# Four graph layers on one core: the second layer's projections as products of rounded halves and rests

## What is computed

```
h = relu(layernorm(x)); x = x + attention(h, adj)            # first layer: q, k, v, softmax
h = relu(layernorm(x)); x = x + gated(h, adj)                # second layer, below
h = relu(layernorm(x)); x = x + (adj != 0) @ (h @ W + b) / deg
h = relu(layernorm(x)); x = x + masked_attention(h, adj)
```

```
hs = h @ W_sa;  s_left = hs @ a_sa[0,:256];  s_right = hs @ a_sa[0,256:]
e = where(adj != 0, exp(-leaky_relu(s_left[:,None] + s_right[None,:], 0.01)), 0)
x_a = (e / (sum(e, 1) + 1e-5)) @ hs
x_b = adj @ (h @ W_gcnb) + b_gcnb
out = sigmoid(alpha_a * x_a + alpha_b * x_b)     # alphas: sigmoids of adj @ h and h times a vector
```

## Time and profile before

| | |
|---|---|
| median of three runs | 398.59 us |
| the profiled execution's own time | 398.4 us |
| its span, first to last instruction | 396.6 us |
| TensorE matmul busy | 384.1 us (97%) |
| TensorE weight load busy | 353.3 us (89%) |
| VectorE busy | 336.8 us (85%) |
| ScalarE busy | 251.8 us (63%) |
| GpSimd busy | 121.8 us (31%) |
| mean granted TensorE clock | 0.998 of full speed |

### The profile page before, as it was taken

One profiled execution on the slowest core, in us unless ns is written; L12 is line 12 of the kernel. 1 busy time (PEld: TensorE's weight loads), 2 busy tenths in 40 slices (PEclk: granted clock), 3 DMA queues, 4 the chain that ended last, 5 costly groups with the idle time before them and its releaser, 6 DMA issues. The chain is left out here.

```text
span 396.6 us, 7768 instructions
## 1 busy us (share of the span) xinstructions
PE 384.1 (97%) x2651; PEld 353.3 (89%) x2651; DVE 336.8 (85%) x771; ACT 251.8 (63%) x531; POOL 121.8 (31%) x130
## 2 busy tenths in 40 slices
PE   7999999999999999999999999999999999999895
PEld 6888888999899899999999899998887898989874
DVE  6898899999984857999999989666888888799893
ACT  3553799888895657876787892255241566267772
POOL 1290000001010424322161011061010599379973
PEclk9999999999999999999999999999999999999999
DMA  8995000000000001000000000000000000010011
GB/s 238 380 382 173 0 0 2 2 0 2 0 2 0 2 1 55 2 2 0 3 2 0 3 0 2 2 1 2 0 2 0 0 2 2 0 55 1 2 54 37
DMA packets 10319, 13.99 MB, mean 35 GB/s; under 512 B 660, under 2 KB 7208, under 8 KB 10280
## 3 DMA queue, kind: packets, MB, share of 16 engines
q1 hardware_dynamic: 9736, 12.96, 9.6%
q10 hardware_dynamic: 544, 0.52, 0.4%
HBM read 12.10 MB, written 1.39 MB: 34 GB/s over the span
## 5 line engine op out<-in xcount | busy, mean ns | idle before, releaser
L1639 PE MATMUL ps<-v_hi,p_hi 128*128 128x258 f32 (+3 forms) x242 | 64.1, 295 | 0.3 <-DVE x_sb L1016 0.2
L402 POOL TENSOR_TENSOR mr_all<-mr_all,mhalf 128x4 f32<-128x4 f32 (+1 forms) x12 | 13.5, 1123 | 162.8 <-DVE mr_all L911 162.8
L1640 PE MATMUL ps<-v_lo,p_hi 128*128 128x258 f32 (+3 forms) x242 | 61.0, 281 | 0.0
L1639 PEld LDWEIGHTS ps<-v_hi,p_hi 128*128 128x128 f32 (+3 forms) x242 | 44.7, 185 | 2.1 <-issue 0.9
L1640 PEld LDWEIGHTS ps<-v_lo,p_hi 128*128 128x128 f32 (+3 forms) x242 | 44.7, 185 | 0.6
L1644 PE MATMUL ps<-v_hi,p_lo 128*128 128x258 f32 (+3 forms) x242 | 40.1, 283 | 1.1 <-DVE p_lo L1192 1.1
L998 DVE TENSOR_TENSOR s_sb<-s_sb,ps 128x512 f32<-128x512 f32 (+3 forms) x63 | 38.3, 610 | 1.3 <-PE ps L1626 1.3
L443 POOL TENSOR_TENSOR mid_lo<-adjT_sb,mid_hi 128x512 fp32r<-128x512 f32 (+2 forms) x16 | 22.6, 1412 | 48.3 <-ACT mid_hi L684 48.3
L1644 PEld LDWEIGHTS ps<-v_hi,p_lo 128*128 128x128 f32 (+3 forms) x242 | 32.5, 185 | 1.7 <-DVE p_lo L1192 1.6
L1931 PE MATMUL ps<-big_hi,p_lo 128*128 128x256 f32 (+3 forms) x121 | 31.8, 294 | 0.6 <-ACT p_lo L867 0.5
L1639 PE MATMUL ps<-big_hi,mid_hi 128*128 128x258 f32 (+3 forms) x121 | 31.8, 294 | 0.0
(11 more groups left out here) (252 smaller groups left out, 1218.1 us busy)
## 6 DMA issues: line engine op xcount, KB each, us to landing
adjT_sb<-in_adjT_dram SPq DMA_DIRECT2D x1, 2816.0 KB, 16.7
adjT_sb<-in_adjT_dram SPq DMA_DIRECT2D x3, 768.0 KB, 8.6
adjT_sb<-in_adjT_dram SPq DMA_DIRECT2D x1, 1815.0 KB, 21.3
out_dram<-x_sb SPq DMA_DIRECT2D x10, 128.0 KB
x_sb<-in_x_dram SPq DMA_DIRECT2D x2, 256.0 KB, 3.6
x_sb<-in_x_dram SPq DMA_DIRECT2D x1, 512.0 KB, 3.9
adjT_sb<-in_adjT_dram SPq DMA_DIRECT2D x1, 512.0 KB, 10.9
rows_sb<-in_rows_dram SPq DMA_DIRECT2D x1, 385.0 KB, 11.1
```

The lines of the kernel that those rows point to most:

```text
L1639: pe.matmul(out_ap, left_[0][0:k, n % RING, mine], right_[0][0:k, j, 0:cols_], start=(j == 0), stop=False)
L1640: pe.matmul(out_ap, left_[0][0:k, n % RING, mine], right_[1][0:k, j, 0:cols_], start=False, stop=False)
```

## The change

The split form replaces `project_full`. `h_hi` and `h_lo`, which the first and fourth layers use, now serve the second layer too: ScalarE writes the rounded half of each turned block into the place where `h_mid` was (`mid_lo`), and VectorE writes the rest into `mid_hi`, where T was. A turn and a projection now wait for the rest (`hlo`) in place of ScalarE's copy. On VectorE the eleven rests stand at step 36 (behind `add_out(1)`, `running` and `stats`), at 38 to 40, at 43 to 46, and in the written-out list. ScalarE splits both weight matrices at step 12, GpSimd writes their rests ahead of `norm(1, 0)`. The first three `adj_hi` wait for projections of h, since they overwrite blocks of rests.

```
--- before.py
+++ after.py
@@ -176,6 +176,7 @@
         rb = sb("rb", [P, NB])
 
         hT0 = [t[:, 0:C * N].rearrange("p (c n) -> p c n", c=C) for t in (big_hi, big_lo)]
+        h1 = [t[:, :].rearrange("p (b c n) -> p b c n", b=NB, c=C) for t in (mid_lo, mid_hi)]
         hT3 = [t[:, :, :].rearrange("p b w -> p (b w)")[:, 0:C * N].rearrange("p (c n) -> p c n", c=C) for t in (v_hi, v_lo)]
         g = [t[:, :].rearrange("p (b w) -> p b w", w=W) for t in (big_hi, big_lo)]
         tT = [t[:, 0:C * N].rearrange("p (c n) -> p c n", c=C) for t in (mid_hi, mid_lo)]
@@ -256,6 +257,8 @@
 
         def h_block(b, layer):
 
+            if layer == 1:
+                return [t[:, b, :, 0:rows(b)] for t in h1]
             return [t[:, :, b * P:b * P + rows(b)] for t in (hT3 if layer == 3 else hT0)]
 
         ps = ctx.enter_context(nc.psum_tensor("ps", [P, 8, BANK], F32))
@@ -285,7 +288,7 @@
             sem(n) for n in ("col_set", "uw_set", "gram_set", "wlr_set", "wext_set"))
         whi, wlo = sems("whi", 7), sems("wlo", 7)
         st, mv, veps, rstd, ln = (sem(n) for n in ("st", "mv", "veps", "rstd", "ln"))
-        zd, zt, hhi, hlo, h_set = (sem(n) for n in ("zd", "zt", "hhi", "hlo", "h_set"))
+        zd, zt, hhi, hlo = (sem(n) for n in ("zd", "zt", "hhi", "hlo"))
         x_add = sems("x_add", 4)
         t_mm, t_hi, t_lo = sems("t_mm", 2), sems("t_hi", 2), sems("t_lo", 2)
         v_mm, vhi, vlo = sems("v_mm", 2), sems("vhi", 2), sem("vlo")
@@ -325,10 +328,7 @@
 
         def h_done(eng, layer, count):
 
-            if layer in (0, 3):
-                wait(eng, hlo, (NB if layer else 0) + count)
-            else:
-                wait(eng, h_set, count)
+            wait(eng, hlo, turns_before(layer) + count)
 
         def products(eng, out_ap, lhs, rhs, first, last):
 
@@ -422,6 +422,14 @@
             pool.wait_ge(half_add, 1)
             for b in range(NB):
                 add_bv(b)
+
+            def weights_rest(k, lo, raw, hi):
+
+                pool.wait_ge(whi[k], 1)
+                pool.tensor_tensor(lo[:, :, :], raw[:, :, :], f(hi[:, :, :]), ALU.subtract).then_inc(wlo[k], 1)
+
+            weights_rest(3, wa_lo, raw_a, wa_hi)
+            weights_rest(4, wb_lo, raw_b, wb_hi)
             norm(1, 0)
             norm(1, 1)
 
@@ -510,13 +518,6 @@
                 act.activation(z_buf[:, b % 4, :], x_sb[:, b, :], ACT.Identity, bias=mr_all[:, b, 0:1],
                                scale=mr_all[:, b, 1:2]).then_inc(zd, 1)
 
-            def h_full(b):
-
-                act.wait_ge(zt, turns_before(1) + b + 1)
-                if b == 0:
-                    act.wait_ge(s_mm[0], NT)
-                act.activation(h_mid[:, b, :, 0:rows(b)], turned(b, 1)[:, :, 0:rows(b)], ACT.Relu).then_inc(h_set, 1)
-
             def z2(b):
 
                 act.wait_ge(ln, NG * 2 + b // PER + 1)
@@ -535,6 +536,8 @@
             def h_hi(b, layer):
 
                 act.wait_ge(zt, turns_before(layer) + b + 1)
+                if layer == 1 and b == 0:
+                    act.wait_ge(s_mm[0], NT)
                 act.activation(h_block(b, layer)[0], turned(b, layer)[:, :, 0:rows(b)], ACT.Relu).then_inc(hhi, 1)
 
             def t_hi_part(gi, a, parts=(0, 1)):
@@ -649,6 +652,14 @@
             for s in range(NB, NT + 13):
                 if s >= 13:
                     exps(s - 13)
+                if s == 12:
+                    act.wait_ge(t_mm[0], 2 * NG)
+                    act.wait_ge(wext_set, 1)
+                    split(3, wa_hi[:, :, :], raw_a[:, :, :])
+                    act.wait_ge(v_mm[0], NB)
+                    act.wait_ge(wg_in, 16)
+                    act.wait_ge(wext_set, 2)
+                    split(4, wb_hi[:, :, :], raw_b[:, :, :])
                 if s == 11:
                     nonzero(1)
                     degree(1)
@@ -660,9 +671,9 @@
                 if 33 <= s < 37:
                     z(s - 33, 1)
                 if s == 35:
-                    h_full(0)
+                    h_hi(0, 1)
                 if 37 <= s < 40:
-                    h_full(s - 36)
+                    h_hi(s - 36, 1)
                 if s == 37:
                     g_row_hi()
                 if 38 <= s < 42:
@@ -670,7 +681,7 @@
                 if 39 <= s < 43:
                     z(s - 35, 1)
                 if 42 <= s < 46:
-                    h_full(s - 38)
+                    h_hi(s - 38, 1)
                     h1_hi(s - 42)
                 if 44 <= s < 46:
                     g_hi(s - 40)
@@ -679,8 +690,8 @@
             def adj_hi(n):
 
                 wait(act, xb_mm, n - 2)
-                if n == 0:
-                    act.wait_ge(s_mm[0], NT)
+                if n < RING:
+                    act.wait_ge(h_mm, 2 * n + 2)
                 act.activation(adj_ring(at[0], n), adj_tile_b(n), ACT.Copy).then_inc(ahi, 1)
 
             def exp1(n):
@@ -738,11 +749,11 @@
             z(9, 1)
             z(10, 1)
             adj_hi(3)
-            h_full(8)
+            h_hi(8, 1)
             adj_hi(4)
-            h_full(9)
+            h_hi(9, 1)
             g_hi(8)
-            h_full(10)
+            h_hi(10, 1)
             exp1(0)
             g_hi(9)
             adj_hi(5)
@@ -913,7 +924,7 @@
             def h_lo(b, layer):
 
                 hi, lo = h_block(b, layer)
-                dve.wait_ge(hhi, (NB if layer else 0) + b + 1)
+                dve.wait_ge(hhi, turns_before(layer) + b + 1)
                 dve.scalar_tensor_tensor(out=lo, in0=turned(b, layer)[:, :, 0:rows(b)], scalar=0.0, in1=f(hi), op0=ALU.max,
                                          op1=ALU.subtract).then_inc(hlo, 1)
 
@@ -1151,8 +1162,14 @@
                     stats(7, 1)
                     for b in range(4, 8):
                         aggr(b, 1)
+                if s == 36:
+                    h_lo(0, 1)
+                if 38 <= s < 41:
+                    h_lo(s - 37, 1)
                 if s == 38:
                     g_row_lo()
+                if 43 <= s < 47:
+                    h_lo(s - 39, 1)
                 if 39 <= s < 43:
                     g_lo(s - 39)
                 if 43 <= s < 47:
@@ -1279,8 +1296,11 @@
             adj_lo(2)
             mask(1)
             ramp(1)
+            h_lo(8, 1)
+            h_lo(9, 1)
             g_lo(8)
             adj_lo(4)
+            h_lo(10, 1)
             g_lo(9)
             mask(2)
             ramp(2)
@@ -1547,12 +1567,6 @@
                                    c == 0, c == C - 1)
                 return ins
 
-            def project_full(out_ap, b, w, n):
-
-                for c in range(C):
-                    ins = pe.matmul(out_ap, h_mid[:, b, c, 0:rows(b)], w[:, c, 0:n], start=(c == 0), stop=(c == C - 1))
-                return ins
-
             def values(b, a):
 
                 layer = 3 if a else 0
@@ -1722,18 +1736,16 @@
             def project_g(b):
 
                 h_done(pe, 1, b + 1)
-                pe.wait_ge(wext_set, 2)
-                pe.wait_ge(wg_in, 16)
+                pe.wait_ge(wlo[4], 1)
                 bank = item("g", b)
-                project_full(ps[0:rows(b), bank, 0:W], b, raw_b, W).then_inc(g_mm, 1)
+                project(ps[0:rows(b), bank, 0:W], b, 1, (wb_hi, wb_lo), W).then_inc(g_mm, 1)
 
             def project_h(b):
 
                 h_done(pe, 1, b + 1)
-                pe.wait_ge(wext_set, 1)
-                pe.wait_ge(wsa_in, 16)
+                pe.wait_ge(wlo[3], 1)
                 bank = item("h", b)
-                project_full(ps[0:rows(b), bank, 0:WA], b, raw_a, WA).then_inc(h_mm, 1)
+                project(ps[0:rows(b), bank, 0:WA], b, 1, (wa_hi, wa_lo), WA).then_inc(h_mm, 1)
 
             def lay_left(gi):
```

More of the change, by code:

```diff
@@ L1548, in project @@
                 return ins
[L1550 to L1554, removed]
             def values(b, a):
```

37 lines of the change are left out of this document (18 added, 19 removed).

## The result

The changed kernel takes 401.36 us (median of 6 runs, 401.06 to 402.53) against 398.59; the ratio is 1.006, 95% interval 1.0032 to 1.0088. It is slower, as forecast, by 2.8 us and not by 1.5. The forecast was 400.1, with 399.5 to 400.9 as its own range and 397.6 to 401.9 for 8 in 10: the measured time lies outside the first and inside the second, next to the 401.9 of *rests in the way*. The profiled execution took 401.08, with a span of 399.0.

The account below looks back on a forecast made before the run. TensorE was taken as the bound from 107 to 129 us. 0.9 + 1.86 + 0.8 + 0.3 - 1.6 - 0.2 + 0.4 - 1.0 = 1.5 on 398.4 gives 399.9, median 400.1; 8 in 10: 397.6 to 401.9.

Parts of the forecast that it names:

- rests in the way: Rival, chance 0.15: VectorE's rests push small operations, turns 5, 6 and 7 wait 0.4 us each as well; 3.3 slower, 401.9.
- Early splits: Weight splits at step 12: ScalarE's copies cost 0.2 to 0.4 us, GpSimd's rests delay VectorE's operations; 0.9 lost in all.
- No locks: Rival, chance 0.20: GpSimd and VectorE miss each other at 51 and 133.33 us; only 0.1 us slower, 398.7.
- First projection to turn 3: Steps 36 onward: late rests on VectorE delay turn 1 by 1.86 us, turn 2 by 0.8 more, turn 3 by 0.3.
- three signs of being wrong: No TensorE wait ahead of the first projection; later turns waiting like the first three; clock falling in 2.3 us of idling.
- Ten projections: g1 to g6 and h0 to h3, up to 129.24 us: each gives back 0.16 us, 1.6 in all.
- The saving does not come: Rival, chance 0.03: on these tiles, or 260 wide, three products take as long as fp32; 3.0 us goes, 403.1.
- a quarter saved: Rival, chance 0.02: a projection takes three quarters of its 0.88 us, 0.66; 1.0 more saved, 399.1.
- Five in a row: Five projections from 129.24 us: would give 0.8 us, but only what shortens VectorE's full chain counts, about 0.2.
- Turn 9: Turn starting at 139.28 us behind ScalarE's copy of block 8: the rest now stands between, plus 0.4 us.
- Last six: Projections g8, g9, g10, h8, h9, h10, between aggregates that TensorE does not wait for: give back 1.0 us.
- Lateness given back: Rival, chance 0.14: VectorE and ScalarE set the pace of steps 39 to 47, turn 3's 3.0 us is made up; 396.9.

## Why the prediction was right, and where its size was off

The sign and the mechanism held: the rests on VectorE delay the first three blocks by more than 22 shorter projections give back. The terms, by the marks of the two spans:

- Early splits, 0.9: measured 0.9, by the kernel with them alone and by the 0.84 at 56.45. ScalarE's part, put at 0.2 to 0.4, is 0.37 by the mark and 0.5 by the medians, at its upper end; GpSimd's is the other 0.4 to 0.5. VectorE's operations met GpSimd's in the way described, the maximum in full (1.20 for 0.69) and `weights_lo` in part (0.81 for 0.69). *No locks* is out.
- First projection to turn 3, 1.86 + 0.8 + 0.3 = 2.96: measured 3.6 (4.5 at turn 3 less the 0.9). **This is the step that was mis-sized.** With full clock it is 3.2 (114.42 less the 110.33 of the earlier trace rows, less 0.9); the missing 0.4 here, 0.6 in the medians, is the clock. The other 0.2 arises ahead of turn 1, which at full clock is 2.05 late where 1.86 was put (110.69 less 107.74, less 0.9). The prediction's last paragraph named the clock as one of three signs of being wrong, and that sign came, 1.3 us behind the idle time; but neither the sum nor a chance had it. The waits were right in kind and near in size: 2.33 put ahead of the first projection (105.47 to 107.80) and 2.30 measured, 0.8 and 0.3 put at turns 2 and 3 and 0.56 and 0.24 measured at full clock. (The start of the rest of block 1, 111.27 in the text, is 111.30 by its own sum of 110.96 and 0.34; it changes nothing.)
- Ten projections, -1.6: measured -1.4 (4.5 to 3.15). A projection takes 0.73 there (132.39 to 133.12), where 0.72 was put. *The saving does not come* and *a quarter saved* are out.
- Five in a row, -0.2: measured -0.45. VectorE's chain up to the rests of aggregate_b(0), which ends this wait, became shorter too: its small operation that took 0.90 beside GpSimd before (133.33) takes 0.65 after, which is the other 0.25.

```profile
136.29 0.65 DVE L921 TENSOR_SCALAR mr_all<-mr_all 128x3 f32<-128x3 f32 x1
```

- Turn 9, +0.4: measured +0.5, with its own wait of 0.45 in the trace.
- Last six, -1.0: measured -0.8.
- *Lateness given back* asked for a turn 4 less than 1.5 us late, the early loss taken off. It was 4.1 - 0.9 = 3.2 late. *Rests in the way* asked for waits of 0.4 at turns 5, 6 and 7; the trace has none of that length, so its 401.9, near the measured time, would have been right for a wrong reason.

The span is 2.4 longer where 1.5 was put: 0.4 to 0.6 by the clock, the rest by terms of 0.2 of either sign. A further 0.3 lies outside of the span: the runs of the changed kernel took 2.1 us around it, and the sum had carried over the 1.8 of the kernel before. 1.5 + 0.9 + 0.3 = 2.7, and the medians differ by 2.8.

The ways out confirm the cause from the other side: where the first three rests are early the kernel gains 2.1 (399.24), where the blocks don't wait for each other in one bank and the splits miss the exponentials, it comes to 397.48. Of the 3.5 us that the 22 projections give, 1.1 to 1.2 then reaches the end.

## What to carry to other kernels

An operation of 0.4 us can cost far more than its own time: what stands ahead of it in its engine's order at that moment counts (here four additions of 1.66 us together). Look up the row it would stand behind, for each of its first instances, and move all of them together, as here one alone only handed its wait to the next. Where all rounds of a loop go through one buffer, an operation added to the chain of a round delays the next one wherever that has no slack (here turns 2, 3 and 9, and none of turns 4, 6 and 7); give those rounds a buffer of their own. When a sum shows an idle gap on TensorE that the kernel did not have, give the clock a term or a chance of its own.

## What was not expected of the hardware

- Idle times of TensorE of nearly one length had different clocks behind them. In the changed kernel it idled 2.30 us up to 108.71, and the clock was at half from 110.0 to 113.5, with TensorE busy again for 1.3 us before it fell. With the splits one step earlier it idled 2.43 up to 108.18, half clock from 109.4 to 112.8. With the fourth product it idled 2.30 up to 108.95, and the clock fell at 108.2, still in the idle time, and was back at 115.0. With the first rest moved it idled 2.21 up to 112.81, and the clock is 1.00 in each window from 109 to 116. Filled with matmuls, 1.00 as well. So a fall can follow such an idle time and does not always; what decides is open.
- Later stages have stretches at half clock in some executions, with TensorE busy, and what they cost differs. In the profiled runs those from 377.8 to 384.6 (first rest moved), 378.7 to 382.1 (filled) and 376.4 to 379.8 (rests early) cost at most 0.3: from turn 10 to the end of the span they take 254.2, 253.9 and 254.0, and the changed kernel, without one, 254.1. The one from 347.0 to 350.4 cost about 0.56. In the runs of the kernel before beside four of the experiments, the four with a mean clock of 0.994 took 399.05 to 399.16, and 24 of the other 25 at most 398.77. Runs of about 3 us more, with mean clocks of 0.978 to 0.982, occur with the first rest moved (four of six), with banks of their own (two of twelve, one of twelve) and in the kernel before (402.44, one of seventeen). None of them was profiled. Why the clock falls there is open; no run varied those stages.
- The time around the span was about 1.8 us in the runs of the kernel before and in those with the splits alone, and 2.1 to 2.2 us in all kernels with the split projections. What adds the 0.3 stays open; the page counts 7774 instructions with the splits alone and 7857 with the split projections.
- VectorE and GpSimd slow each other: both operations can come out longer (GpSimd 1.78 and 1.76 for 1.09, VectorE 1.20 and 1.64 for 0.69), by who started first.
